# Key tile 7's probabilities join key tile 6's on VectorE, and the softmax denominators are summed from one buffer instead of two

## The reference

```
xn = layernorm(x)
q, k, v = rope(xn @ Wq), rope(xn @ Wk), xn @ Wv     # 16 heads of q, 64 wide; k and v made for 8 and repeated
scores  = softmax(q @ k / 2, axis=-1)               # 4 batches x 16 heads x 1024 queries x 1024 keys
attn    = (scores @ v) @ Wo
ffn     = (silu(xn @ wg.T) * (xn @ wu.T)) @ wd.T
out     = x + attn + ffn
```

## Time and profile before

| | |
|---|---|
| time, median of 3 runs | 1212.84 us (1211.01 to 1213.59) |
| the profiled execution | 1210.01 us, its span 1208.2 us |
| PE busy | 1161.2 us, 96% of the span |
| DVE busy | 892.1 us, 74% |
| POOL busy | 878.2 us, 73% |
| ACT busy | 697.7 us, 58% |
| mean granted TensorE clock | 0.989 |
| chain that ended last | PE 90%, DVE 3%, POOL 2%, ACT 1% |

### The profile page before, as it was taken

How to read it: one execution, slowest core, us unless ns; L and a number is a source line. 1 busy time by engine, 2 the same in 40 slices (tenths; PEclk the granted TensorE clock), 3 DMA queues, 4 the chain that set the end, 5 groups by cost and what they waited for, 6 DMA issues and landing times.

```text
span 1208.2 us, 19402 instructions
## 1 busy us (share of the span) xinstructions
PE 1161.2 (96%) x6288; PEld 642.0 (53%) x6288; DVE 892.1 (74%) x1009; ACT 697.7 (58%) x1074; POOL 878.2 (73%) x274
## 2 busy tenths in 40 slices
PE   5898999999999999999999999999999999999985
PEld 4786455555555555555555555555555555554432
DVE  7685778777777778777777777777777777876622
ACT  3333556666666656666666656666666556665563
POOL 2312777887778877787777887787777887787775
PEclk9898999999999999999999999999999999999997
DMA  6652707062421517062422517061422517050000
GB/s 222 172 238 99 213 2 217 1 188 65 142 76 62 156 36 215 0 197 55 141 75 74 143 36 215 0 202 49 148 68 87 131 36 215 0 125 1 4 1 17
DMA packets 56287, 124.58 MB, mean 103 GB/s; under 512 B 7968, under 2 KB 19488, under 8 KB 54048
## 3 DMA queue, kind: packets, MB, share of 16 engines
q1 hardware_dynamic: 56224, 123.89, 35.0%
HBM read 53.08 MB, written 10.49 MB: 53 GB/s over the span
## 4 chain that ended last, share of the span: by engine, by line
PE 90%; DVE 3%; POOL 2%; ACT 1%; issue 1%; DMA 1%; SPq 1%; POOLq 0%; ACTq 0%; DVEq 0%
PE bank_s L542 24%; PE scores L379 22%; PE bank_o L394 20%; PE scores L362 7%; PE bank_m L370 3%; PE bank_m L404 3%; PE bank_m L430 2%; PE bank_m L407 2%; POOL prob_sum L1018 2%; PE scores L480 2%; PE bank_s L497 1%; PE bank_m L414 1%; PE bank_m L421 1%; DVE prob L917 1%; DMA x_all<-x 1%
## 5 line engine op out<-in xcount | busy, mean ns | idle before, releaser
L824 DVE TENSOR_REDUCE row_max<-scores 128x1 f32<-128x1024 f32 x512 | 605.7, 1217 | 194.7 <-PE scores L379 194.7
L1018 POOL TENSOR_TENSOR prob_sum<-prob_sum,prob 128x2048 f32<-128x2048 f32 x128 | 586.3, 4581 | 112.9 <-DVE prob L917 103.8
L542 PE MATMUL bank_s<-qk_pack 98*128 98x512 f32 x1024 | 383.6, 432 | 12.8 <-ACT prob L768 6.7
L779 ACT ACTIVATE prob<-bank_s 128x512 f32<-128x512 f32 x512 | 285.1, 596 | 172.3 <-PE bank_s L542 165.1
L768 ACT ACTIVATE prob<-bank_s 128x1024 f32<-128x1024 f32 x256 | 262.5, 1025 | 187.8 <-PE bank_s L542 180.5
L379 PE MATMUL scores<-qk_pack 96*128 96x512 f32 x1024 | 340.5, 419 | 1.1 <-DVE row_max L824 1.1
L542 PEld LDWEIGHTS bank_s<-qk_pack 98*128 98x128 f32 x1024 | 183.0, 189 | 232.4 <-ACT prob L768 144.3
L394 PE MATMUL bank_o<-prob,v 128*32 128x512 f32 x2048 | 273.6, 606 | 0.9 <-ACT prob L779 0.9
L379 PEld LDWEIGHTS scores<-qk_pack 96*128 96x128 f32 x1024 | 177.0, 190 | 136.8 <-DVE row_max L824 109.1
L963 POOL TENSOR_TENSOR qk_stage<-rope,qk_stage 128x512 fp32r<-128x512 f32 x64 | 82.1, 1283 | 90.8 <-ACT qk_stage L653 90.8
L1011 POOL TENSOR_TENSOR prob_sum<-prob 128x2048 f32<-128x2048 f32 x32 | 146.4, 4575 | 0.0
(11 more groups left out here) (88 smaller groups left out, 679.5 us busy)
## 6 DMA issues: line engine op xcount, KB each, us to landing
qk_pack<-qk_stage SPq DMA_DIRECT2D x384, 128.0 KB, 3.5
table<-tables SPq DMA_DIRECT2D x16, 2048.0 KB, 9.9
w_stage<-w_scratch SPq DMA_DIRECT2D x14, 640.0 KB, 4.7
v<-v_stage SPq DMA_DIRECT2D x32, 256.0 KB, 3.2
xT_scratch<-xT_hl SPq DMA_DIRECT2D x4, 1024.0 KB, 9.5
x_stage<-xT_scratch SPq DMA_DIRECT2D x4, 1024.0 KB, 5.4
w_scratch<-w_split SPq DMA_DIRECT2D x1, 2560.0 KB, 15.1
x_all<-x SPq DMA_DIRECT2D x4, 512.0 KB, 12.5
```

The source lines that it names most:

```text
L542: mm(bank_s[:, h % 2, :], qk_pack[j][0:SCORE_K, 1, kt // QT, h, (kt % QT) * 128:(kt % QT + 1) * 128], qk_pack[j][0:SCORE_K, 0, t, h, :], s ...
L779: A(prob[:, kt % RING, h, :], bank_s[:, h % 2, :], ACT.Exp).then_inc(prob_ready, 1)
L824: V.tensor_reduce(row_max[:, m:m + 1], scores[:, at:at + 2, :].rearrange("p c k -> p (c k)"), axis=AX.X, op=ALU.max).then_inc(max_read, 1)
L1018: TT(prob_sum[:, t], prob_sum[:, t], prob[:, kt % RING], ALU.add).then_inc(sum_done, 1)
```

## The change

VectorE gets a new instruction, `last_pair_sum(u)`: it adds the probabilities of key tile 7 into the buffer of key tile 6, 128 partitions x 2048 elements. It stands in the next unit, behind the reduction of tile `m` = 1, or, in the last unit, which has no maxima, ahead of `invert`; for unit 31 it stands behind everything else. GpSimd's last addition of a unit, which takes the buffer of tile 6, now waits for it (`last_done`) and so takes in tile 7 as well. TensorE's denominators lose the four products of tile 7 with the ones; the four with `prob_sum` both start and end the group. Key tile 3 of the next unit, which overwrites the buffer of tile 7, waits for VectorE's addition instead of TensorE's denominators. Nothing else is changed.

```
@@ denominators (TensorE)
                 pe.wait_ge(v_staged, capped(u + 5, UNITS))
-                for h in range(HG):
-                    mm(bank_m[h * E:(h + 1) * E, :], ones[:], prob[:, (KT - 1) % RING, h, :], start=True, stop=False)
                 pe.wait_ge(sum_done, 5 * u + 5)
                 for h in range(HG):
-                    last = mm(bank_m[h * E:(h + 1) * E, :], ones[:], prob_sum[:, t, h, :], start=False, stop=True)
+                    last = mm(bank_m[h * E:(h + 1) * E, :], ones[:], prob_sum[:, t, h, :], start=True, stop=True)
                 last.then_inc(den_ready, 1)
@@ slot (ScalarE)
                         elif kt == 3:
-                            act.wait_ge(den_ready, u)
+                            act.wait_ge(last_done, u)
@@ VectorE
+            def last_pair_sum(u):
+
+                dve.wait_ge(prob_ready, NE * (KT * u + 8))
+                dve.wait_ge(pv_done, 8 * u + 7)
+                V.tensor_tensor(prob[:, 6 % RING], prob[:, 6 % RING], prob[:, 7 % RING], ALU.add).then_inc(last_done, 1)
@@ slot (VectorE)
                     for m in range(TILES):
                         reduce_tile(u + 1, m)
+                        if m == 1 and not is_first(u):
+                            last_pair_sum(u - 1)
                         if m == INVERT_AFTER and not is_first(u):
                             invert(u - 1)
                     split_max(u + 1)
                 else:
+                    last_pair_sum(u - 1)
                     invert(u - 1)
...
             pairs_of_steps(dve, body)
+            last_pair_sum(UNITS - 1)
             invert(UNITS - 1)
             normalise(UNITS - 1)
@@ add_probs (GpSimd)
                     if kt == 4:
                         pool.wait_ge(pair_done, u + 1)
+                    elif kt == 6:
+                        pool.wait_ge(last_done, u + 1)
                     else:
                         pool.wait_ge(prob_ready, NE * (KT * u + kt + 1))
```

More of the change, by code:

```diff
@@ L180, in build @@
             sem("denT_ready"), sem("inv_done"), sem("inv_spread"), sem("inv_ready"))
+        last_done = sem("last_done")
         o_done, y_ready, y_read, y_added = sem("o_done"), sem("y_ready"), sem("y_read"), sem("y_added")
```

## The result

| | before | after |
|---|---|---|
| median of the timed runs | 1212.4 us (1211.0 to 1213.6, 4 runs) | 1298.2 us (1297.0 to 1302.3, 4 runs) |
| profiled execution | 1210.0 us | 1297.4 us |

The changed kernel takes 1.0714 times as long, 95% interval 1.0687 to 1.0741. It is slower, by 85.8 us; the forecast was 67.5 us and its range ended at 1298.0. So the sign was right and the size was short by 18 us.

What follows compares the result with a forecast made beforehand. TensorE, busy 96% of the span, was taken as the bound. 54.6 + 1.5 + 3.5 + 5.4 + 0.2 + 2.3 = 67.5 us on the profiled 1210.0 gave 1277.5, or 1280 against timed runs; range 1254 to 1298.

Steps and rivals of the forecast that it cites:

- the path and its place: VectorE's late addition delays GpSimd's last addition, ScalarE's key tile 2 and TensorE's scores; TensorE 1.54 us late a unit.
- Rival B: The wait at ScalarE's key tile 2 stays, but the cast costs nothing: 1.54 us a unit, 1262 us; chance 0.15.
- Rival D: VectorE's addition is hidden in its free time, needing a start 1.8 us into the unit: 1186 us; chance 0.04.
- Rival C: Only the late reductions on VectorE cost TensorE time: 0.9 us a unit, 1240 us; chance 0.06.
- Rival E: ScalarE's small waits at key tiles 0 and 4 are passed on: 0.6 us more in 27 units, 1296 us; chance 0.15.
- The removed products: TensorE's products of key tile 7 with the ones, expected to save 0.86 us a unit.
- the cast and the next start: VectorE's cast held by GpSimd's addition adds 0.5 us a unit; ScalarE's key tile 0 waiting for GpSimd adds 0.06.
- units 2 to 27: The 26 units priced at 2.1 us each: 54.6 us.
- unit 31 and the end: 0.2 us for unit 31, which has no maxima, and 2.3 for GpSimd's additions behind it, delayed by VectorE's.
- run only when GpSimd is between instructions: VectorE's 16-number cast and its two-buffer addition were said to stand still until GpSimd's running instruction ends.
- What TensorE loses: The step counting TensorE's removed instructions: 0.86 us a unit in 30 full units, 26 us less.
- the clock adds nothing: TensorE's clock was expected to stay at the 2.4 GHz level, with TensorE idle some 3 of 36 us a unit.

Runs made afterwards that it cites:

- short_pool: loop_moved_filled with GpSimd's addition of key tile 3 cut to 16 columns: 1259.5 us, ratio 1.0389.
- loop_moved_filled: The changed kernel with 64 useless TensorE instructions ahead and five useless products a unit in the wait before maximum tile 4: 1281.0 us, ratio 1.0572.
- no_handover: The changed kernel with 64 useless TensorE instructions ahead; VectorE's addition goes to the other buffer and GpSimd doesn't wait for it: 1280.1 us, ratio 1.057.
- before_moved: The kernel before with 128 useless TensorE instructions put ahead of everything: 1222.8 us, ratio 1.0098.
- behind_3: The changed kernel with 64 useless TensorE instructions ahead and VectorE's addition behind reduction 3 instead of 1: 1421.9 us, ratio 1.1729.
- ahead_spread: ahead_moved with maximum tile 2 moved on TensorE from key tile 0 to key tile 1, ahead of the output projection: 1226.9 us, ratio 1.0129.
- ahead_late2: ahead_moved with maximum tile 2 behind the first two scores of key tile 1 on TensorE: 1208.1 us, ratio 0.9967.
- ahead_moved: The changed kernel with VectorE's addition ahead of all reductions and 64 useless TensorE instructions ahead of everything: 1216.0 us, ratio 1.0037.
- no_handover_filled: no_handover with five useless TensorE products a unit in the wait ahead of maximum tile 4: 1261.8 us, ratio 1.0415.

## Why the prediction was right, and where it failed

**Right: the path and its place.** VectorE's addition behind reduction 1, GpSimd's start, ScalarE's key tile 2, TensorE's scores: each came within 0.1 us of the forecast (table above). Freed of the two effects below, the kernel takes 1281.0 us in units of 36.0, against 1280 in units of 36.0; over the kernel before beside it that is 69.6 us, against 67.5. Rival B is out: the cast is held (short_pool). Rival D is out, by its own point: the addition started 4.4 us into the unit, not 1.8. Rival C's 0.9 us a unit is what remains without the hand-over, in the units whose clock stays up. Rival E is out as well, although its 1296 us lie next to the 1298.2: without code and clock the units are 36.0, not 36.6, so that nearness would have been luck.

**Nearly right: sizes.** The removed products measured 0.82 us a unit instead of 0.86, the cast and the next start 0.4 instead of 0.56. These two nearly cancel. In the profile of loop_moved_filled units 2 to 27 are 53.8 us longer than before (forecast 54.6), units 1, 28, 29 and 30 together 10.9 (10.4), but unit 31 and the end 5.3, and for these the sum had 0.2 + 2.3. In unit 31 a part of it is the clock, which stayed up in the kernel before; the windows, before and then loop_moved_filled:

```profile
1160.00:1190.00 30.00, 24.79 (x135) 9.46 (x134) 5.70 (x3) 19.90 (x30) 23.77 (x6) 1.00 0.00 1
```

```profile
1226.00:1256.00 30.00, 25.98 (x126) 10.38 (x125) 8.74 (x5) 18.22 (x28) 22.65 (x6) 0.89 0.00 1
```

The prediction also read from the held cast that the two lines "run only when GpSimd is between instructions". For GpSimd's additions this held; beside its subtractions it is too strict. In no_handover VectorE's addition, begun 1.54 us ahead of GpSimd's subtractions, overlapped with them and took 2.86 us, and they took 3.67.

**Failed: the sum had no term for code.** The step that failed is "What TensorE loses": it counted the removed instructions' time and not their place, so that the jumps back of TensorE's loop stood in the sum at nothing, without a reason. 14.4 us (1298.2 - 1283.8) are five jumps that now wait for code. VectorE, GpSimd and the semaphore have no part in it: before_moved pays the same way with only the place changed. The Trainium skill, Runtime: NRT & Kernel Launch, section Instruction fetch mechanics, gives TensorE room for 2048 instructions, filled in blocks of 16 KiB (256 instructions), and says that a taken branch whose target isn't in the current 2-page window stalls the engine. The trace agrees on the block (1.06 MB in 65 packets) and on the stall at the jump. It does not agree on two pages: the kernel before jumps back over 1668 instructions, more than six blocks, and loads nothing again (21 packets). By the 2048 alone both loops (1668 and 1604) would stay loaded, and the runs show that the shorter one does not where 2438 stand ahead of it.

**Failed: "the clock adds nothing".** I read it from unit 31, where TensorE idles 16% of the time at granted 1.00, as if the idle share decided. The forecast itself had a wait of 1.65 us at one place in each unit. The falls come behind that wait, in one unit of two to three. Here they cost 2.8 us net by the medians, which is no more than their intervals allow for nothing; in no_handover they cost 18.3, clear of the noise.

Both sum up: 67.5 forecast, + 14.4 code, + 2.8 clock, + 1.1 of rest = 85.8 us. In the rest the 2.8 us of unit 31 and the end stand against 0.8 less in units 2 to 27 and against the two medians of the kernel before (1212.4 and 1211.4).

**The expectations that missed** (no_handover, both filled kernels, behind_3, ahead_spread, ahead_late2) mostly priced the wait that the edit touched and left out what came next: the clock, a collision or GpSimd's path in the last units. In loop_moved_filled it was the other way, the clock was priced too high. before_moved and ahead_moved missed by 1 us.

## What to carry to other kernels

Before a product is taken from the bounding engine, follow what replaces it to the place where that engine meets it again: here 0.8 us was bought with a 7-us path (VectorE 2.3, GpSimd 4.6) that another engine waits for at a fixed place, and the place in VectorE's order, three lines, was worth 72 us. Compare the packets of the instruction queue before and after any edit of an engine's long loop; if they triple, put some instructions ahead of the loop and time it again before the edit is judged. Where a forecast has the bounding engine wait over 1 us in one piece, price the clock as well.

## What the runs showed of the hardware

- Whether TensorE's loop stays loaded depends on where it begins: with 2485, 2500 or 2502 instructions ahead of it there were 21 packets, with 2438 and 2613 there were 65 and 67, at passes of 1604 to 1668 instructions. Which rule decides it stays open. A unit with a jump that misses is 1.3 to 2.9 us longer than the others (before_moved, after).
- TensorE's clock fell to the 1.2 GHz level for some 3 us behind single waits of 1.5 to 2.1 us in full units. Not behind each: in no_handover the waits of 1.46 us passed and those of 1.9 to 2.1 did not, but for one; in after ten of the 17 waits of 1.5 to 1.6 us at the maximum tile had a fall behind them. Useless products in the wait kept it up and made no_handover 18.3 us (1.4%) faster.
- VectorE's addition of two buffers took 2.28 us alone, 2.7 to 2.9 us beside GpSimd's 512-column subtractions (no_handover_filled); beside one of 2.86 us two of these took 3.67 us instead of 2.52 (no_handover). So both engines pay.
- A cast of 16 numbers a row takes 175 ns and took up to 2.4 us where an addition of GpSimd was running (after, short_pool).
